# Mixing matmuls placed between the query banks of a strip's tail, the variance matmuls in two parts, and the FFN's second flip ahead of the feature matmuls

## What is computed

```python
x = x + _L0_conv_ref(_ln_c(x), ...)            # halo attention
t = _to_tokens(x)
t = t + _L0_ffn_ref(_ln_t(t), W1, b1, W2, b2)  # fp8 products, fp16 sums
x = _from_tokens(t, x)
x = x + _L1_conv_ref(_ln_c(x), ...)            # clusters: similarity, gather, mix
t = _to_tokens(x)
t = t + _L1_ffn_ref(_ln_t(t), W1, b1, W2, b2)
```

## Time and profile before

| | |
|---|---|
| median of 3 runs | 9042.88 us (9035.99 to 9101.01) |
| the profiled execution | 9053.59 us |
| its span in the trace | 9051.6 us |
| mean granted TensorE clock | 0.899 |
| busy: PE, PEld, DVE, ACT, POOL | 87%, 70%, 76%, 54%, 28% |
| full steps | 36 to 127, from 2233.14 us to some 8245 us of the span |

### The profile page before, as it was taken

How to read it: one execution, slowest core, us unless ns; L and a number is a source line. 1 busy time by engine, 2 the same in 40 slices (tenths; PEclk the granted TensorE clock), 3 DMA queues, 4 the chain that set the end, 5 groups by cost and what they waited for, 6 DMA issues and landing times.

```text
span 9051.6 us, 429211 instructions
## 1 busy us (share of the span) xinstructions
PE 7854.1 (87%) x172050; PEld 6323.5 (70%) x172050; DVE 6910.7 (76%) x22530; ACT 4896.1 (54%) x9750; POOL 2503.7 (28%) x4860
## 2 busy tenths in 40 slices
PE   6999999998899899988989889998898989897555
PEld 4777777777777777777777777777777777775433
DVE  3676777877888887777887778777888778887666
ACT  2444444545555565555655555555565555655445
POOL 1333333333333323223232223322323223332000
PEclk7998999989999999999999999999999999998555
DMA  2111111111222222222222222222222222221111
GB/s 57 40 42 42 44 51 46 51 51 54 58 61 57 57 60 56 61 58 55 61 64 55 56 58 58 55 59 58 57 58 62 57 54 61 58 61 53 56 54 60
DMA packets 193342, 501.73 MB, mean 55 GB/s; under 512 B 33508, under 2 KB 67108, under 8 KB 191468
## 3 DMA queue, kind: packets, MB, share of 16 engines
q1 hardware_dynamic: 191692, 476.75, 19.3%
HBM read 228.84 MB, written 169.93 MB: 44 GB/s over the span
## 4 chain that ended last, share of the span: by engine, by line
PE 69%; DVE 15%; issue 9%; ACT 6%; DMA 1%; SPq 0%; ACTq 0%; DVEq 0%; POOL 0%; POOLq 0%
PE scores_x L703 10%; PE bank L662 6%; PE flipped L725 6%; PE pv L753 4%; PE bank L665 4%; DVE maxes L1570 3%; PE bank L673 3%; PE misc L616 3%; PE bank L962 3%; PE pv L747 3%; PE scores_x L643 3%; PE bank L607 3%; PE misc L782 3%; DVE shifted L1578 2%; PE bank L680 2%
## 5 line engine op out<-in xcount | busy, mean ns | idle before, releaser
L2046 POOL TENSOR_TENSOR vrest<-vstage,vmask 96x384 f32<-96x384 f32 x512 | 437.6, 855 | 4615.4 <-ACT vstage L1199 4615.4
L1570 DVE TENSOR_REDUCE maxes<-scores_x 128x6 f32<-128x864 f32 x1024 | 1076.8, 1052 | 780.1 <-PE scores_x L703 775.6
L703 PE MATMUL scores_x<-keys,queries 64*64 64x144 f32 x24576 | 1070.7, 307 | 133.3 <-DVE shifted L1578 66.5
L665 PE MATMUL bank<-xn,wq 97*32 97x64 f32 x24576 | 961.8, 233 | 138.9 <-issue 137.8
L662 PE MATMUL bank<-xt,wq 97*32 97x64 f32 x24576 | 941.9, 233 | 127.1 <-issue 115.0
L703 PEld LDWEIGHTS scores_x<-keys,queries 64*64 64x64 f32 x24576 | 786.8, 142 | 378.5 <-issue 343.3
L662 PEld LDWEIGHTS bank<-xt,wq 97*32 97x32 f32 x24576 | 814.9, 118 | 262.3 <-issue 237.8
L1578 DVE TENSOR_TENSOR shifted<-scores_x,maxes 128x768 f32<-128x768 f32 x1024 | 969.4, 947 | 0.5
L665 PEld LDWEIGHTS bank<-xn,wq 97*32 97x32 f32 x24576 | 828.5, 117 | 151.9 <-issue 151.8
L1187 ACT ACTIVATE queries<-bank 128x512 f32<-128x512 f32 x768 | 458.8, 597 | 864.6 <-PE bank L665 862.4
L725 PE MATMUL flipped<-ident,shifted 128*128 128x128 f32 x6144 | 895.3, 284 | 0.2 <-ACT vstage L1199 0.2
(11 more groups left out here) (193 smaller groups left out, 17382.9 us busy)
## 6 DMA issues: line engine op xcount, KB each, us to landing
keys<-kst SPq DMA_DIRECT2D x768, 99.0 KB, 3.6
x_in<-x_dram SPq DMA_DIRECT2D x130, 396.0 KB
xn_kept<-xn SPq DMA_DIRECT2D x128, 388.0 KB, 2.5
later<-xn_kept SPq DMA_DIRECT2D x128, 388.0 KB, 3.4
x_tok<-tok_dram SPq DMA_DIRECT2D x128, 384.0 KB, 3.1
x_kept<-x SPq DMA_DIRECT2D x128, 384.0 KB, 2.4
later<-x_kept SPq DMA_DIRECT2D x128, 384.0 KB, 3.6
out_dram<-later SPq DMA_DIRECT2D x128, 384.0 KB, 2.4
```

The source lines that it names most:

```text
L665: last = mm(dst[64 * e + 32:64 * e + 64, :, j, :], wq[0:PROW, 2 * WS + j, 2 * g + e, :], rows[:, j], start=True, stop=True, skip_group_che ...
L703: last = mm(score[e][64 * j:64 * j + 64, g * NKEY:(g + 1) * NKEY], queries[64 * e:64 * e + 64, g, w, :], keys[64 * e:64 * e + 64, g, :, WS ...
L1570: V.tensor_reduce(maxes[:, p % 2, :, :], sc, AX.X, ALU.max).then_inc(max_ready.sem, 1)
```

## The change

PE: the two mixing matmuls leave p == 5 and stand in the tail, the first between query banks 1 and 2, the second between query banks 3 and `project(1)`. They write `fill` (the banks of `flipped`) instead of `work`, after ACT has emptied these banks of `hidden_c(n, 4)` and `(n, 5)`; the waits of `spread` and of the query banks for `mixed` fall away, and `make_values(n+1, 1)`, which uses `fill` next, gets one. The heads' second flip moves one query bank back. `mean(n+1, 1)` moves behind `flip(0)`. `flip_z(n-1, 1)` moves ahead of the features. Two of the three variance pieces move from p == 3 to p == 2, between `weigh(1)` and `hidden(n-1, 2)`.

DVE: the two additions of the mixing leave p == 6 and stand in the tail, behind `hidden_c(n, 5)` and ahead of `best_of` (which ends in `simw`). `ffn_apply(n-1, 1)` moves from p == 2 to the end of p == 1, ahead of tile 2's maximum.

ACT: `store_z(n-1, 1)` moves ahead of the third square and the squared features; the last two `quantise` of the first network move ahead of `store_sims`.

In `drain` the mixing stays in `work` at its old place.

```diff
@@ PE, make_queries
-                elif on and on.c1:
-                    pe.wait_ge(mixed.sem, mixed.at(n - 1, i + 1))
@@ PE, attend: ahead of flip(p)
                     if p == 0:
                         if on.c3:
                             pe.wait_ge(hc_evac.sem, hc_evac.at(n - 1, 6))
+                        if on.c2:
+                            pe.wait_ge(mixed.sem, mixed.at(n - 1, 2))
                         make_values(n, 1, fill)
                     if p == 0 and ahead:
                         pe.wait_ge(v_stored.sem, v_stored.at(n, 2))
                         mean(n + 1, 0)
-                        mean(n + 1, 1)
+                    if p == 2 and b1:
+                        if on.b:
+                            pe.wait_ge(ft_ready.sem, ft_ready.at(n, 2))
+                        flip_z(n - 1, 1)
                     if p == 2 and on.b:
...
                     if p == 3 and ahead:
-                        for c in range(3):
-                            variance(n + 1, c, on)
+                        variance(n + 1, 2, on)
...
                     if p == 6:
                         flip_heads(0)
-                        if on.c1:
-                            pe.wait_ge(mixed.sem, mixed.at(n, 2))
@@ PE, attend: behind flip(p) and weigh(p - 1)
                     if p == 0:
+                        if ahead:
+                            mean(n + 1, 1)
...
-                    if p == 2 and b1:
-                        if on.b:
-                            pe.wait_ge(ft_ready.sem, ft_ready.at(n, 2))
-                        flip_z(n - 1, 1)
+                    if p == 2 and ahead:
+                        variance(n + 1, 0, on)
+                        variance(n + 1, 1, on)
...
                     if p == 5:
                         if b2:
                             pool(n - 2)
-                        if on.c1:
-                            pe.wait_ge(v_stored.sem, v_stored.at(n, 8))
-                            mix(n, 0)
-                            mix(n, 1)
@@ PE, attend: the tail
-                    make_queries(n + 1, 1, on)
+                    make_queries(n + 1, 1)
+                if on.c1:
+                    if on.c2:
+                        pe.wait_ge(hc_evac.sem, hc_evac.at(n, 5))
+                    mix(n, 0, fill)
+                if ahead:
+                    make_queries(n + 1, 2)
                 flip_heads(1)
                 if ahead:
-                    make_queries(n + 1, 2)
                     make_queries(n + 1, 3)
+                if on.c1:
+                    if on.c2:
+                        pe.wait_ge(hc_evac.sem, hc_evac.at(n, 6))
+                    mix(n, 1, fill)
                 project(1)
@@ ACT, attend
                     if p == 2:
+                        if b1:
+                            store_z(n - 1, 1)
...
                     if p == 2 and b1:
-                        store_z(n - 1, 1)
...
                     if p == 4:
+                        if b1:
+                            quantise(n - 1, 4)
+                            quantise(n - 1, 5)
                         if on.c1:
                             store_sims(n)
                         if b1:
-                            quantise(n - 1, 4)
-                            quantise(n - 1, 5)
@@ DVE, attend
                     if p == 1 and b1:
                         ffn_normalise(n - 1, 1, False, on.c2)
-                    if p == 2 and b1:
                         ffn_apply(n - 1, 1)
...
                     if p == 6:
-                        if on.c1:
-                            mix(n, 0, par)
-                            mix(n, 1, par)
...
                 if on.c2:
                     hidden_c(n, 4)
                     hidden_c(n, 5)
+                if on.c1:
+                    mix(n, 0, par, fill)
+                    mix(n, 1, par, fill)
                 if on.b:
                     best_of(n)
```

22 lines of the change are left out of this document (11 added, 11 removed).

## The result

The changed kernel takes 9118.13 us (9080.03 to 9141.78, 7 runs) where the kernel before takes 9036.45 us (9023.78 to 9101.01, 7 runs). The ratio is 1.0076, 95% interval 1.0041 to 1.0111: slower by 0.8%, where I had forecast 8750 us. The profiled execution has a span of 9112.1 us against 9051.6, 60.5 us more: 37.4 lie ahead of step 36, 20.5 in the full steps 36 to 126 and 2.6 behind them.

What follows compares the result with a forecast made beforehand. It took PE's list with its idle places as the bound. From 9053.6 us profiled, 138 for the moved work and 156 for the clock came off, giving 8760, stated as 8750 after allowing for the runs' median; range 8600 to 8965.

Steps and rivals of the forecast that it cites:

- Part 1: Mixing out of p == 5: PE gets 1.4 us back, the wait of spread 0.3; sum -1.7 us a full step.
- Part 2: Mixing into the tail on PE: 1.4 us of work absorbed by idle time in the query banks; 0 taken.
- R2: Rival: the mixing is not absorbed in the tail, which grows by 1.4 us; 8960 us, chance 0.13.
- Part 4: Flip ahead of features, ffn_apply ahead of tile 2: 0.78 becomes a wait of scores(3), 0.64 is gained; -0.6 us a step.
- Part 3: Mixing into the tail on DVE: its 1.10 us of additions stand ahead of simw; +0.8 us a full step.
- R3: Rival, slower: the gather waits for DVE's tail and this pause makes the clock fall; 9300 us, chance 0.07.
- R4: Rival: scores(3) waits for DVE some 0.5 us longer than PE gained; 46 us off the forecast, within its 0.62.
- Part 5: Variance in two parts: no work added, no further gain at output(1), whose wait is 1.0 us a step; 0 taken.
- Part 6: The clock in full steps: of 4.9 us lost a third, 1.7, comes back, mostly in the tail; -156 us.
- The early steps: Steps 1 to 35, with parts 4 and 5 alone: -0.6 to +0.6 us each, at most 20 us; 0 taken.
- The sum without the clock: Parts 1 to 5 over a full step: -1.5 us, in 92 steps -138 us.
- The signs I named: Expected in the changed profile: certain waits gone or new, clock 0.95 to 0.97; wrong if warmest steps not below 60.5 us.

Runs made afterwards that it cites:

- e2_mix_only: The kernel before with the mixing's part of the change alone (with store_sims behind the two quantisations); 8778.57 us, ratio 0.9705.
- e8_mix_tiny: e2_mix_only with PE's two mixing matmuls cut to 4 of their 384 columns; 8854.28 us, ratio 0.9772 to the kernel before.
- e4_mix_late: e2_mix_only with DVE's two mixing additions behind best_of and residual(1); ratio 0.971 to the kernel before.
- e6_pool_less: The changed kernel with POOL normalising one stream tile of eight, seven left out; 8700.68 us, ratio 0.9628 to the kernel before.
- e10_pool_order: The changed kernel with POOL's mask_values(n, 1) and repeat_rest(n, 3) ahead of normalise_stream(n - 2); 8837.48 us, ratio 0.9741 to the kernel before.
- e16_best_var: e10_pool_order plus e18_after_early's early steps, one repeat of the transposes of flip_features(n, 1), and the variance in one part; 8613.44 us, ratio 0.9545 to the kernel before.
- e1_ffn_back: The changed kernel with ffn_apply, flip_z(n - 1, 1) and store_z(n - 1, 1) at their old places; 8904.36 us, ratio 0.9826 to the kernel before.
- e5_mean_late: e2_mix_only with mean(n + 1, 1) behind the first tile's flips; ratio 0.9688 to the kernel before.
- e14_ffn_only: e2_mix_only with ffn_apply, flip_z and store_z at their new places, mean and variance as before; ratio 0.9831 to the kernel before.
- e18_after_early: The changed kernel with flip, ffn_apply and variance put back in steps 0 to 17, the mean alone in 18 to 35; ratio 1.003 to the kernel before.
- e13_sims_late: The kernel before with ACT's store_sims moved behind the fifth tile's two quantisations; 8979.19 us, ratio 0.9942.
- e12_dummy_tail: The kernel before with the two mixing matmuls issued again in the tail, unread, and the heads' second flip one bank later; 9035.18 us, ratio 0.9958.

## Why the prediction was wrong, step by step

**Where it was right.** *Part 1*, the mixing out of p == 5: its 1.4 us on PE and the wait of `spread` are gone; with the reordered `store_sims` the way from `output` to the first query bank is 2.4 us shorter (18.9 to 16.5 in e2_mix_only). *Part 2*, absorption: the tail from the first query bank on takes 13.3 us, 13.2 before, with two matmuls more in it; the idle in the banks is 110.6 us by its two rows, against 186.2 by the earlier trace rows and the row below, and in e8_mix_tiny it grows again when the matmuls are cut. So R2 falls. *Part 4* in its first half: the 0.78 us ahead of `output_c` turned into a wait of `scores(3)`.

```profile
PE bank L662 <- issue: 86.1, 82, 2.4
```

**Part 3 was mis-sized, without effect.** I let DVE's 1.1 us stand ahead of `simw`; it is 2.2 with the wait for PE's second matmul, which I had not ordered against DVE's. I priced it at 0.8 us. e4_mix_late shows 0: what it delays is late on ACT's side as well. R3's mechanism (gather waits for DVE) is there at 0.47 us a step, below its own bound of 1 us, and the clock does not fall there.

**Part 4 failed in the price of `ffn_apply`.** "Its 1.16 us" is the row of its old place. At the new one it is 2.3 us in the mean, because POOL's additions and its mask product run there (e6_pool_less and e10_pool_order, with these out of the way, bring it back to 1.1 and 1.2). So R4 was true at 1.79 us a step, not 0.5. The trace of before had it. This is POOL in step 84 of the kernel before; the new place begins at 5414.81, behind the last root step:

```profile
5415.00 0.87 POOL L2065 TENSOR_TENSOR xn_half<-xn 128x388 f32<-128x388 f32 x1 [0.18 <-POOL xn L2059]
5416.05 0.53 POOL L2069 TENSOR_TENSOR xn_sum<-xn_half 128x194 f32<-128x194 f32 x1 [0.18 <-POOL xn_half L2065]
5416.54 0.84 POOL L2046 TENSOR_TENSOR vrest<-vstage,vmask 96x384 f32<-96x384 f32 x1
```

The prediction does not mention POOL, since nothing waits for it. The Trainium skill (SBUF — State Buffer, Who interferes with whom) states that a DVE instruction with two SBUF inputs contends with a POOL instruction that reads SBUF, that one in a mode that uses both ports contends with any of POOL's, and that whichever starts first blocks the other for its whole length. The trace agrees for POOL's two-input instructions (L1476, which has two inputs, 180 ns alone and 847 beside L2053; L1717 902 beside L2072); beside POOL's one-input L2066 the same two mostly take 205 and 332 ns, which the rule does not separate. By that rule alone the move would have been priced at up to the length of POOL's instructions there, an estimate of 2.2 us by the three rows above.

**Part 5 was not 0, in two of its terms.** The variance in two parts makes no difference once the wait is short (e16_best_var), but with the flip at its old place it costs 1.4% (e1_ffn_back against e5_mean_late). Beside the longer wait, and with the mean moved, it is part of the 2.5% between e14_ffn_only and the changed kernel; which of the two does it there was not run, but in the steps 18 to 35 the mean alone costs 2.4 us a step (e18_after_early). And `output`'s wait, for which I took 0, was worth 0.99 us a full step by `store_sims` alone (e13_sims_late).

**Part 6 failed in its sign.** The tail's clock came back (2.4 to 0.2 us a step) and gave little, as e12_dummy_tail shows: I had read the slow tail of step 89 as the price of the clock, and more of the time at the lower level is in the middle (3.5 us a step, 2.4 in the tail). There I let smaller pieces "lean towards a higher clock" and did not ask what the new wait of `scores(3)` would do, although show the clock at 0.63 in step 89, which has a wait of 0.64 us for ACT's `z8t` just ahead, like step 84:

```profile
5749.37 0.38 PE L927 MATMUL flipped<-z8t,w1q 96*128 96x512 fp8e5 x1 [0.64 <-ACT z8t L1306]
```

R3 had the right mechanism, a new pause that makes the clock fall, at the wrong place: I looked for it at the gather and not at the wait that my own part 4 had just made.

**The early steps** I had at 0 and at most 20 us; they cost some 40 (e18_after_early, by intervals that just overlap). Part 4 has the wait of `scores(3)` there too, and the prediction took its gain and loss as even.

**The sum without the clock**, -1.5 us a full step, did not come either: the 18 steps of the changed kernel that ran at full clock throughout take 61.89 us in the mean, and the 5 of the kernel before 61.98. What parts 1 and 5 gave, the wait of `scores(3)` took.

The signs I named: DVE's wait for the mixing gone (it is 149.1 us, moved and not gone), idle in the banks below 1 us a step (1.2, from 2.0), ACT's z8t gone (yes), `scores(3)` half a us (1.79), clock 0.95 to 0.97 (0.93). By the clock alone, which I had named as what would make me wrong, the prediction fell. The steps at full clock are at 61.9 us; only two of them are below 60.5.

## What to carry over

When an instruction is moved, take its duration from what else touches the memory at the new place, on engines that nobody waits for too: here one of DVE's took 902 ns beside POOL's addition and 326 alone. Do not price a wait by its length alone: filling a wait of 1.8 us with useless work made the kernel 4.3% faster, because the clock no longer fell behind it. Of two kernels with the same sum of waits, the one with 0.75 and 1.20 us in two places ran 2.5% faster than the one with 0.16 and 1.79, though the variance's place differs too. And take a change of several parts apart before judging it: this one held one of 3% gain and one of nearly 3% loss.

## What the runs showed of the hardware

- Useless matmuls in front of a wait made a kernel 4.3% faster, and matmuls cut to a hundredth of their columns made one 0.7% slower. The features' sixteen matmuls took 1.99 us at 2.4 GHz and 3.70 where the granted clock of the stretch was 0.59; over the full steps of the changed kernel one has a mean of 369 ns against 278.
- The time at the lower level does not grow in proportion to the wait: 0.6 us behind 0.53, 3.1 behind 1.20, 7.6 behind 1.79 (each a mean over the full steps). Behind waits of 0.3 it is 0.9 to 2.0, so another cause is at work as well.
- PE's pauses without a semaphore stand whole multiples of 256 of its instructions apart (all 131 of 0.4 us or more in the query banks of the kernel before, but for three jumps). So where instructions come late depends on how many there are: eight more than 2685 matmul and load records a step took 1.5% off, whichever of the two places they had. The Trainium skill (Runtime: NRT & Kernel Launch, Instruction fetch mechanics) has the crossing of a 16 KiB block as mostly hidden; here 0.6 to 2.1 us a step was not.
- DVE's maxima and subtraction, which read PSUM, and its batch statistics (one SBUF input, 228 to 253 ns for one of L1684 with POOL at work or not) were not slowed by POOL. But one SBUF input is no protection: of two instructions that have one, L1717 went from 326 to 902 ns, and L1875 (128x512, f16) from 345 alone to 1226 beside POOL's copies L2026 and L2035.
